# Softmax attention in a fused four-layer kernel: the output product taken from unsplit fp32 probabilities, two column halves of the array at once, with three rotating score buffers

## The reference: what is computed

```python
HEADS, HALF, HEAD_DIM = 16, 16, 32          # b, s = 2, 1024
q = (q_latent @ wq_u).reshape(b, s, HEADS, HALF)
k = (kv_latent @ wk_u).reshape(b, s, HEADS, HALF)
v = (kv_latent @ wv_u).reshape(b, s, HEADS, HEAD_DIM)
q = q * cos + _rotate_half(q) * sin
k = k * cos + _rotate_half(k) * sin
attn = jnp.einsum('bqhd,bkhd->bhqk', q, k) * scale
attn = jax.nn.softmax(attn, axis=-1)
out = jnp.einsum('bhqk,bkhd->bqhd', attn, v)
return out.reshape(b, s, d) @ wo
```

## Time and profile before

| | |
|---|---|
| median of three runs | 2998.82 us (2996.97 to 3001.64) |
| profiled execution | 3001.32 us, of which the span from first to last instruction is 2999.5 us |
| attention heads, first exponential to the last division | 1753.7 to 2379.4 us of the span |
| PE busy over the whole span | 2800.3 us (93%) |
| DVE, ACT, POOL busy over the whole span | 1709.0 us (57%), 1076.6 us (36%), 788.0 us (26%) |

### The profile page before, as it was taken

How to read it: one execution, slowest core, us unless ns; L and a number is a source line. 1 busy time by engine, 2 the same in 40 slices (tenths; PEclk the granted TensorE clock), 3 DMA queues, 4 the chain that set the end, 5 groups by cost and what they waited for, 6 DMA issues and landing times. The chain is left out here.

```text
span 2999.5 us, 37368 instructions
## 1 busy us (share of the span) xinstructions
PE 2800.3 (93%) x13738; PEld 2220.9 (74%) x13738; DVE 1709.0 (57%) x2590; ACT 1076.6 (36%) x1624; POOL 788.0 (26%) x832
## 2 busy tenths in 40 slices
PE   7966988799999999999999679999999999999998
PEld 7845787678888888888888546666666678888886
DVE  6864677664545544454553666666666456546554
ACT  3343333221121111111211457777777522212221
POOL 0038676200000000000000147777887600000000
PEclk9967899899999999999999879999999999999999
DMA  2242232210000100000100032111111000101001
GB/s 85 105 116 68 56 73 49 51 38 22 22 21 22 41 21 21 21 21 21 33 10 1 30 97 57 54 55 55 56 53 47 29 15 29 43 1 42 14 15 42
DMA packets 102052, 123.60 MB, mean 41 GB/s; under 512 B 50400, under 2 KB 77280, under 8 KB 100256
## 3 DMA queue, kind: packets, MB, share of 16 engines
q1 hardware_dynamic: 101920, 121.86, 14.0%
HBM read 94.55 MB, written 26.74 MB: 40 GB/s over the span
## 5 line engine op out<-in xcount | busy, mean ns | idle before, releaser
L2101 POOL TENSOR_TENSOR att_p_lo<-att_probs,att_p_hi 128x768 fp32r<-128x768 f32 x256 | 465.7, 1836 | 142.1 <-ACT att_p_hi L2164 141.3
L2270 DVE TENSOR_REDUCE att_top<-att_q_scores 128x1 f32<-128x1024 f32 x250 | 305.7, 1223 | 214.8 <-PE att_q_scores L2380 213.4
L284 DVE TENSOR_TENSOR fp_hidden<-fp_gelu,fp_up 128x512 f32<-128x512 f32 x128 | 88.1, 688 | 442.0 <-PE fp_up L75 379.0
L2175 ACT ACTIVATE att_probs<-att_k_scores 128x1024 f32<-128x1024 f32 x256 | 263.4, 1029 | 151.3 <-PE att_k_scores L2399 151.2
L1819 POOL MEMSET lat_power<- 128x16 f32 x1 | 0.1, 112 | 1049.9 <-POOLq L52 1049.9
L343 ACT ACTIVATE fp_gelu<-fp_gate 128x512 f32<-128x512 f32 x128 | 76.4, 597 | 420.0 <-PE fp_gate L75 419.2
L270 DVE TENSOR_TENSOR k_stream<-k_stream,fp_down 128x512 f32<-128x512 f32 x256 | 175.5, 686 | 89.5 <-PE fp_down L75 86.0
L2164 ACT CAST att_p_hi<-att_probs 128x768 fp32r<-128x768 f32 x256 | 212.2, 829 | 0.0
L73 PE MATMUL fp_gate<-fp_feat_hi,fp_w_hi 128*128 128x512 f32 x512 | 200.6, 392 | 3.8 <-DVE fp_feat_lo L258 3.8
L74 PE MATMUL fp_gate<-fp_feat_lo,fp_w_hi 128*128 128x512 f32 x512 | 200.0, 391 | 0.0
L75 PE MATMUL fp_gate<-fp_feat_hi,fp_w_lo 128*128 128x512 f32 x512 | 200.0, 391 | 0.0
(11 more groups left out here) (360 smaller groups left out, 6540.8 us busy)
## 6 DMA issues: line engine op xcount, KB each, us to landing
f_early<-codes SPq DMA_DIRECT2D x16, 768.0 KB
f_early<-scales SPq DMA_DIRECT2D x16, 768.0 KB
att_q_stack<-rotated SPq DMA_DIRECT2D x192, 64.0 KB, 2.6
att_k_stack<-rotated SPq DMA_DIRECT2D x192, 64.0 KB, 2.7
la_values<-w_sparse SPq DMA_DIRECT2D x10, 1024.0 KB, 5.1
f_early<-qkv SPq DMA_DIRECT2D x16, 576.0 KB, 6.1
qkv<-f_early SPq DMA_DIRECT2D x12, 512.0 KB, 2.8
k_stream<-hidden SPq DMA_DIRECT2D x4, 1024.0 KB, 10.2
```

Of the source, the lines that this page charges most:

```text
L284: dve.tensor_tensor(hidden[:, c, :], gelu[:, c, :], up_ps[c][:], ALU.mult).then_inc(product_done, 1)
L2101: pool.tensor_tensor(p_lo[:, buffer, :], probs[:, slot, 0:SPLIT], p_hi[:, buffer, :].bitcast(F32), ALU.subtract).then_inc(lo_done, 1)
L2175: act.activation(probs[:, t, :], k_scores[:], ACT.Exp).then_inc(exp_done, 1)
L2270: dve.tensor_reduce(top[buffer][:, STACK + t:STACK + t + 1], scores[:], AX.XY, ALU.max, negate=True).then_inc(max_done, 1)
```

## The change

- The probabilities are no longer split. `output` now issues two fp32 matmuls for a tile, each with all 512 queries of one half of the sequence, against the same 64 columns of `padded` (32 values, a column of ones, zeros). The first writes partitions 0 to 63 of the PSUM tile `out`, the second partitions 64 to 127, so each uses one half of the columns of the array and all its rows. The rounding on ACT, the subtraction on POOL, `split_values`, `whole_values`, `fold` and the second PSUM copy go.
- `turn_out` makes 4 transposes of 128 columns in place of the 8 matmuls with `fold`.
- Query and key scores share three PSUM buffers, `scores[0..2]`, in rotation. `query_scores` runs AHEAD = 15 tiles ahead and waits for the exponential that last read its buffer; `key_scores` waits for the maximum that last read its buffer.
- The order of PE is a new one (`outputs_of_step`, and the loop at the end of the diff). POOL now pads the values and does the rotation of `project_piece` from a copy in SBUF, which ACT makes. SP loads the stacks of a head before it places the top row of the next, and not after.

```diff
-SPLIT = 768
 PROBS = QTILES
-OUT_ROWS = 2 * HEAD_DIM1 + 2
-OUT_COLS = HEAD_DIM1 + 1
-AHEAD = QTILES + 4
-BEHIND = 3
+AHEAD = 2 * QTILES - 1
 PIECE = SEQ // QUAD
 PREPARED = 2
...
-        split_values = s.sb("split_values", [P, 2, QTILES, P], F32R)
-        whole_values = s.sb("whole_values", [P, 2, QTILES, P])
+        padded = s.sb("padded", [P, 2, QTILES, VALUE_COLS])
         probs = s.sb("probs", [P, PROBS, SEQ])
-        p_hi, p_lo = s.sb("p_hi", [P, 4, SPLIT], F32R), s.sb("p_lo", [P, 4, SPLIT], F32R)
-        out_t = s.sb("out_t", [P, SEQ])
-        fold = s.sb("fold", [P, OUT_COLS])
-        inverse = s.sb("inverse", [P, QTILES])
-        q_scores, k_scores = s.ps("q_scores", [P, 2, TB]), s.ps("k_scores", [P, 2, TB])
-        out_rest, late = s.ps("out_rest", [P, 2, TB]), s.ps("late", [P, 2, TB])
-        out_first, turned = late[:, 0, :], late[:, 1, :]
-        piece = turned
+        out_t = s.sb("out_t", [P, TB])
+        inverse = s.sb("inverse", [P, 2, QUARTERS1])
+        scores = [s.ps(f"scores{b}", [P, 2, TB]) for b in range(3)]
+        out, turned = s.ps("out", [P, TB]), s.ps("turned", [P, TB])
+        product = scores[1:]
+        rot_hi, rot_lo = s.sb("rot_hi", [P, PREPARED, SEQ], F32R), s.sb("rot_lo", [P, PREPARED, SEQ], F32R)
+        piece = s.sb("piece", [P, 2 * PIECE])
...
+        def query_bank(tile):
+            return scores[2 * (tile - AHEAD) % 3]
+
+        def key_bank(tile):
+            return scores[(2 * tile - 1) % 3]
...
+                if g and g + QUAD - 1 < HEADS:
+                    sp.wait_ge(b_done, T * g)
+                    to, slot = divmod(g + QUAD - 1, QUAD)
+                    if slot == 0 and to >= PREPARED:
+                        wait_stored(sp, QUAD * (to - PREPARED) + QUAD - 2)
+                        wait_stored(sp, QUAD * (to - PREPARED) + QUAD - 1)
+                    load(to, slot)
...
-            def low(at, slot, buffer):
-                pool.wait_ge(hi_done, at + 1)
-                pool.tensor_tensor(p_lo[:, buffer, :], probs[:, slot, 0:SPLIT],
-                                   p_hi[:, buffer, :].bitcast(F32), ALU.subtract).then_inc(lo_done, 1)
...
+            def pad_values(g):
+                if g >= 2:
+                    pool.wait_ge(out_done, T * (g - 1))
+                pool.tensor_copy(padded[:, g % 2, :, 0:HEAD_DIM1], values_of(g)).then_inc(padded_done, 1)
...
+            for g in range(HEADS):
+                if g + 1 < HEADS:
+                    pad_values(g + 1)
+                if has_piece(g // QUAD):
+                    rotate_piece(g)
+                    low_piece(g)
...
+            def copy_piece(k):
+                act.wait_ge(piece_ps, k + 1)
+                if k:
+                    act.wait_ge(piece_lo_done, k)
+                act.copy(piece[:], turned[:]).then_inc(piece_copied, 1)
...
-            def high(at, slot, buffer, first):
-                act.wait_ge(exp_done, at + 1)
-                if not first:
-                    act.wait_ge(out_done, at - 3)
-                act.copy(p_hi[:, buffer, :], probs[:, slot, 0:SPLIT]).then_inc(hi_done, 1)
...
+            def exponential(tile):
+                act.wait_ge(b_done, tile + 1)
+                if tile >= PROBS:
+                    act.wait_ge(out_done, tile - PROBS + 1)
+                act.activation(probs[:, tile % PROBS, :], key_bank(tile)[:], ACT.Exp).then_inc(exp_done, 1)
...
-                scores = (late, k_scores)[j] if prologue and t % 2 else q_scores
-                if not prologue:
-                    pe.wait_ge(max_done, T * g + t)
-                elif T * g + t >= 2:
-                    pe.wait_ge(max_done, T * g + t - 1)
+                if tile > AHEAD:
+                    pe.wait_ge(exp_done, tile - AHEAD)
+                elif tile >= 3:
+                    pe.wait_ge(max_done, tile - 2)
...
-                if not (first and t == 0):
-                    pe.wait_ge(exp_done, T * g + t)
+                if tile - 2 + AHEAD < STEPS:
+                    pe.wait_ge(max_done, tile - 1 + AHEAD)
+                else:
+                    pe.wait_ge(exp_done, tile - 2)
...
-            def output(g, buffer, t, first):
-                at = T * g + t
+            def output(tile):
+                g, t = divmod(tile, T)
                 if t == 0:
-                    pe.wait_ge(v_lo_done, g + 1)
-                    pe.wait_ge(v_whole_done, g + 1)
-                    if not first:
-                        pe.wait_ge(copied_act, g)
-                        pe.wait_ge(copied_dve, g)
-                pe.wait_ge(hi_done, at + 1)
-                for part, done in ((p_hi, None), (p_lo, lo_done)):
-                    if done:
-                        pe.wait_ge(done, at + 1)
-                    start, stop = t == 0 and part is p_hi, t == T - 1 and part is p_lo
-                    pe.matmul(out_first, split_values[:, buffer, t, :], part[:, t % 4, 0:TB], start=start, stop=stop)
-                    pe.matmul(out_rest[:, 0, 0:REST], split_values[:, buffer, t, :], part[:, t % 4, TB:], start=start, stop=stop)
-                pe.matmul(out_rest[:, 1, 0:REST], whole_values[:, buffer, t, :], probs[:, t, SPLIT:],
-                          start=t == 0, stop=t == T - 1).then_inc(out_done, 1)
-
-            def turn_out(g, first):
-                if not first:
+                    pe.wait_ge(padded_done, g + 1)
+                    if g:
+                        pe.wait_ge(out_copied, g)
+                pe.wait_ge(exp_done, tile + 1)
+                for half in range(2):
+                    rows = copy_rows(half)
+                    last = pe.matmul(out[rows, :], padded[:, g % 2, t, :], probs[:, t, half * TB:(half + 1) * TB],
+                                     start=t == 0, stop=t == T - 1)
+                last.then_inc(out_done, 1)
+
+            def turn_out(g):
+                if g + 2 < HEADS:
+                    pe.wait_ge(top_copied, g + 3)
+                if has_piece((g + 1) // QUAD):
+                    pe.wait_ge(piece_copied, g + 2)
+                if g:
                     pe.wait_ge(mixed_done, g)
-                pe.wait_ge(copied_act, g + 1)
-                pe.wait_ge(copied_dve, g + 1)
-                for t in range(T):
-                    last = pe.matmul(turned[:, t * OUT_COLS:(t + 1) * OUT_COLS], out_t[:, t * P:(t + 1) * P], fold[:],
-                                     start=True, stop=True)
+                pe.wait_ge(out_copied, g + 1)
+                for t in range(QUARTERS1):
+                    last = pe.transpose(turned[:, t * P:(t + 1) * P], out_t[:, t * P:(t + 1) * P], ident[:])
                 last.then_inc(out_turned, 1)
...
+            def outputs_of_step(g, t):
+                behind = ((-3,), (-2, -1), (), (0,), (1,), (2,), (3,), (4,))[t]
+                return [T * g + tile for tile in behind if T * g + tile >= 0]
...
+            for tile in range(AHEAD):
+                query_scores(tile)
+                if tile == T - 1:
+                    turn_top(0)
+            key_scores(0)
+            for g in range(HEADS):
+                for t in range(T):
+                    step = T * g + t
+                    if step + AHEAD < STEPS:
+                        query_scores(step + AHEAD)
+                    if t == 1 and g + 1 < HEADS:
+                        turn_top(g + 1)
+                    if t == 2 and has_piece(g // QUAD):
+                        project_piece(g)
+                    if t == 5 and g:
+                        turn_out(g - 1)
+                    for tile in outputs_of_step(g, t):
+                        output(tile)
+                    if step + 1 < STEPS:
+                        key_scores(step + 1)
+            for tile in (STEPS - 3, STEPS - 2, STEPS - 1):
+                output(tile)
+            turn_out(HEADS - 1)
 
 
```

More of the change, by code:

```diff
@@ L2086, in _ @@
                     store_piece(n, j)
-                if n + 1 < PASSES:
-                    sp.wait_ge(b_done, T * (g + 1))
-                    if j == 0 and n and not has_piece(n):
-                        wait_stored(sp, QUAD * n - 1)
-                    load(n + 1, j)
                 if g == QUAD * (PASSES - 2) + 1:
@@ L2116, in _ @@
-            pool.memset(split_values[:].bitcast(F32), 0.0).then_inc(values_zeroed, 1)
-            pool.memset(whole_values[:], 0.0).then_inc(values_zeroed, 1)
-            for x in range(PREPARED):
-                pool.wait_ge(stored[x], 32)
-            low_values(0, 0, 0)
-            def body(n, first, last):
-                for j in range(QUAD):
-                    g = QUAD * n + j
-                    for t in range(T):
-                        low(T * g + t, t, t % 4)
-                        if t == 5 and not (last and j == QUAD - 1):
-                            low_values(g + 1, n + (j + 1) // QUAD, (j + 1) % QUAD)
@@ L2266, in maximum @@
-            def maximum(g, buffer, t, first, scores=q_scores):
-                if t == 0 and not first:
+            def maximum(tile):
```

(18 more changed lines are left out.)

287 lines of the change are left out of this document (100 added, 187 removed).

## The result

| | before | changed |
|---|---|---|
| median | 3000.23 us (2996.97 to 3006.28, 4 runs) | 2851.35 us (2849.66 to 2853.56, 4 runs) |
| ratio | | 0.950, 95% interval 0.949 to 0.952 |
| span of the profiled execution | 2999.5 us | 2851.8 us |

The changed kernel is 5.0% faster, 149 us, where 126 were forecast. The direction, the bound and the mechanism were as predicted; the sum of the gains was 15% too small.

A forecast was written before the change was run, and what follows sets the result against it. PE was taken as the bound, with no idle time in a step. Gains of 90 (first 24 heads) + 33 (last 8) + 5 (tail) - 2 (start) = 126 us off 3000 gave 2874; own range 2853 to 2925, chance 0.68.

The forecast's parts named there:

- the halves run at once: Output matmuls of a tile: the two column halves overlap fully, 0.85 us for a tile against 1.71 without overlap.
- The serial rival: Output matmuls: column halves run one after another, 1.71 us a tile, 3093 us in all; chance 0.14.
- Mode change 0.20: PE going from row halves of the scores to the whole array and back: 0.20 us each, 8 groups a head, 1.6.
- step 1: Step of a head with `turn_top` and two outputs on PE: 2.87 us.
- Step 5: Step of a head that also holds `turn_out` on PE: 2.32 us.
- The wait of 0.1 for the copy: First output of a head: PE waits 0.1 us for the copy of `out`.
- The last 8 heads: Heads without a piece: 15.4 us each, PE reaching the copy 1.1 too early; 118 against 151.6, gain 33.
- The collision with `low_weights`: Last 8 heads of before: `low_weights` ahead of `copy_top` on DVE while POOL works; three heads lose some us each.
- 2 lost: Ahead of the first exponential: three more tiles of query scores, 1.22 us each, less a covered DVE wait, lose 2 us.
- Tail: Behind the last exponential: 10.5 us falls to 5.6, gain 5.
- What lies beside PE: Other engines in a head: ACT falls to 9.8 us and DVE to about 11, so neither binds at 15.5.
- The low end, 2853: Whole kernel: low end of the forecast's own range, with 11 us won on weight loads and 10 on waits at the copy.

The follow-up runs named there:

- all columns: Changed kernel with the values padded to 128 columns, so both output matmuls of a tile use the whole array and add into the whole PSUM tile: 3074.88 us.
- the second trace of before: The kernel of before, unchanged, profiled once more in another execution: 2996.37 us.
- another order in the last 8 heads: Changed kernel with the previous head's last two outputs put one in step 1 and one in step 2 of the last 8 heads: 2851.00 us.
- 60 and 5 matmuls: Changed kernel plus unused 128-column identity matmuls, 60 behind the first projections and 5 behind each early tile of query scores: 2862.05 us.
- The other order on DVE: Kernel of before with the `low_weights` subtraction of the last four heads moved behind the copy of the top rows, one reduction later: 2991.81 us.

## Where the prediction was right, and which step failed

- **The bound, and that the halves run at once**: right. Two records start together at 1868.17, and an output takes 1.01; with both in one column half it takes 1.86, the 0.85 of two more passes, and the kernel is slower than before. The serial rival had worked out 3093 for that case, 219 above its forecast; the run lies 218 above the changed kernel. That the two agree to 1 us is in part luck: one head of the run still has its halves at once, and its start is 4.8 later.
- **The cited rule**: the section of the Trainium skill ("TensorE: Matmul & The Clock Gate", "Part 3: Packing small matmuls — row/col tiling") has weights loading under a running matmul only when the row groups differ. That column halves would be serial by it was my inference: the rule speaks of weight loads alone, and the same section lists three column tiles at 2.38 times the speed of one by one. This case's trace doesn't bear the rule out, since all four weight loads of an output are over within 0.20 us of its start, while its first two matmuls run for 0.65 on the same rows:

```profile
1868.16 0.20 PEld L2339 LDWEIGHTS att_out<-att_probs,att_padded 128*64 128x64 f32 x4 [0.36 <-issue]
```

Two column halves here stream at twice the speed of one by one: 0.86 us for an output (1.01 less 0.15 of mode change) against 1.71 (1.86 less 0.15). The figure for three was met by no run.

- **Mode change 0.20**: the step that failed. The price was taken from weights of 128 columns. With 64 columns a group that holds an output exposes 0.05 less, so an ordinary step is 1.67 and not 1.72, and the runs with one column half and with all columns show the same 0.05 (1.86 against 1.91). A head has seven such groups, which is 0.35 of the 0.54 us by which it is shorter than forecast, and 11 us in all. The prediction had exactly these 11 us, but as an upside and not in its sum.
- **The other steps of the head**: step 1 was to take 0.67 + 0.20 + 1.70 + 0.3 = 2.87 and takes 2.76; 0.07 of this is `turn_top`, which takes 0.23 (1858.24 to 1858.47) and not 0.3. Step 2 was 1.58 and is 1.57. Step 5 was 2.32 and is 2.26, `turn_out` 0.59 as said. The wait of 0.1 for the copy isn't there. Together 0.25 + 0.11 + 0.01 + 0.06 + 0.10 = 0.53, the 15.5 that became 14.96. Over 24 heads that is the 13 us missing. All these differences have one sign.
- **The last 8 heads**: 15.4 forecast, 14.85 measured. Most of it is the same 0.35 and 0.07. The wait for ACT is 0.65 and stands at the query scores, where 1.1 was forecast at line 2339, but the scores behind it lose time too, so waits make only about 0.1 of the difference. The collision with `low_weights` was right as a mechanism, worth 8 us; it hit two heads and not three.
- **The start**: the "2 lost" for three more tiles was about right, 1.5 by the traces. From the first query scores to the first exponential there are 19.2 us (1731.10 to 1750.25), and 17.6 in both traces of before. What the prediction lacked is that the first stacks arrive 1.5 sooner, which by the rows is because DVE no longer builds `fold` ahead of the first rotation (no run shows it by itself); in the trace of before this stands there:

```profile
1716.60 1.86 DVE L2222 COPY att_fold<-k_ident 32x32 f32<-32x32 f32 x2
```

So from the last rounding of the latents (line 1841, ahead of the heads) to the first exponential there are 47.4 us in both traces, and the 3.5 us in the table lie ahead of it: they are the execution, as the second trace of before shows. In the run with another order in the last 8 heads, whose code is the same up to there, they are 49.0, with a granted clock of 0.57 from 1709 to 1717.

- **Tail**: 5 forecast, 4.9 measured.
- **What lies beside PE**: right, and now with prices. In a head with a piece no wait shows. ACT's old work brought back costs 51 us, and two buffers cost 35: the room beside PE was there, and the 8 x 0.83 = 6.6 us of rounding in a head would have more than filled it.
- Without the 3.5 us of the start the terms measured are 144, of which the prediction had 126: 13 in the first heads, 4 in the last 8, 2 at the start, less 0.7 behind the heads.
- **The low end, 2853**, was the forecast less two upsides, 11 for the mode changes and 10 for the waits. The first came true in full and the second in part; `turn_top` and the start took the time below it. The 1.65 us by themselves are less than the 4.9 by which the start of the heads moves between two executions of one kernel, so on which side of 2853 the median falls is chance. The shortfall of 18 us in the heads and at the start isn't.

## What to carry to other kernels

Two fp32 matmuls that share their rows and use different column halves of the array ran fully at once here, so two unsplit fp32 products of 64 columns stream in the time of one; look for products whose weights fill only half the columns before splitting operands. When PE gets faster, check each partner's loop for the new step: here a third score buffer (35 us) and ACT's dropped rounding (51 us) were conditions of the full gain. A term that the change itself makes smaller, such as the load of half as many weight columns, belongs in the sum and not among the upsides; if the small terms all carry a margin on the dear side, the sum is a bound and not a forecast.

## What the runs showed of the hardware

- Weights of 64 columns (fp32) expose 0.05 us less than 128 behind the 64-row scores (1.86 against 1.91 for the output). Beside whole-array matmuls it is the other way round: four transposes and the output behind them take 0.59 + 1.86 with 64 columns and 0.50 + 1.81 with 128.
- The granted clock was 0.50 for 20 us while PE was busy 97% of the time with matmuls and small waits between them, and in another run for 10 us with PE busy in all of them; with 60 and 5 matmuls it was 1.00 over 10 us in which PE was as busy. In the first two PE had waited before the clock fell, 3.8 us and 2.3 us, though one wait of 2.1 us passed without a fall. What decides was not settled.
- Two waits of 1.6 us on PE went with a loss of 8 us in the kernel of before. The waits are 3.1 of it; the granted clock of the stretches around them (0.86, 0.91 and 0.89 in three windows of 15 us from 2295 on) makes the other 5.1, an estimate from the missing shares. The other order on DVE took both away.
